# Autocorrelation by spectra: weights at plain delays, outputs as even and odd parts, and a new order of ScalarE's and TensorE's calls

## The chip, the cores and the metric

The kernel runs on one core of a Trainium2 chip. The metric is device microseconds of one execution, the median over several. TensorE does the matrix products and writes to PSUM; VectorE and ScalarE read PSUM and SBUF; GpSimd (POOL) works on SBUF only; SyncE (SP) issues the transfers. Each engine runs its own queue of instructions in order, and waits on semaphores where the program says so.

## The reference, cut to what matters

Two blocks in a row, each an attention-like step and a feed-forward step with a gate, over x of shape (8, 256, 1024). The change touches the second attention step only, an autocorrelation over time, on the normed x as query and on the context as key and value:

```python
corr = ifft(fft(q, axis=time) * conj(fft(k, axis=time))).real
topk = int(2 * np.log(L))                    # L = 256, topk = 11
w, idx = jax.lax.top_k(corr.transpose(0, 1, 3, 2), topk)
w = softmax(w)
for i in range(topk):
    g = jnp.minimum(idx[:, :, None, :, i] + pos, L - 1)
    out = out + w[:, :, None, :, i] * take_along_axis(v, g, axis=2)
x = x + tanh(g_xattn[1]) * out
x = x + tanh(g_ffn[1]) * ffn(layernorm(x))    # a 1024x1024 linear with a gain
```

For each channel the 11 largest correlations over the 256 delays become softmax weights, and the output is the value series, weighted at those delays. The shift is not circular: past the end the last value stands.

## The kernel before, in words

X (the running x) lies in SBUF in 16 tiles of 128 time rows by 1024 channels; a batch is two tiles, and the rows of its second tile are stored in reverse. With that, cosine and sine transforms over 256 time points split into a sum part and a difference part of 128 rows each.

The last phase, `phase_tail`, holds the second attention step and the last linear layer. It cuts the attention into N = 16 units (8 batches, two halves of 512 channels). Its main loop runs n from 0 to N + LAG - 1 = 18. In step n, unit n is at its output, unit n+1 at its correlation and selection, unit n+2 at its query and key spectra, and unit n+3 at its key's fold; beside these, tile `nxt` = n-2 of X is normed and turned and tile `now` = n-3 goes through the linear layer. Each engine has its own list of calls for a step; these lists are the order, written out by hand.

The calls that matter, by engine:

- TensorE (list at L1438 to L1466): `weight_turn(n)` transposes the softmax weights into psC (L1379); `linear(now, 0)` is 24 f16 matmuls of 512 columns (L1427); `weight_even(n)` takes the even spectrum of the weights, six f16 matmuls (high and low parts, L1338); `corr(n+1)`, 16 f32 matmuls of 256 columns (L1372); `weight_odd(n)`; `linear(now, 1)`; `turn(nxt, 0)`, four transposes into the first bank of psL (L1413); `k_odd(n+1)`, two f32 matmuls of 512 columns (L1334); `output(n)`, eight f32 matmuls of 512 columns from four sources into the two banks of psQ (L1401); `k_even(n+2)`; `turn(nxt, 1)` into the same bank of psL as the first turn; `q_spectrum(n+2)` into psQ (L1338). A f32 matmul shows as two records.
- VectorE (L1594 to L1628): `products(n+1)`, `weights_low(n)`, statistics, `weight_products(n, 0)` (e_d, e_x), `gain_of(now, 0)`, `weight_products(n, 1)` (n_d, n_x, L1572 and L1573), `select(n+1)` (the 11 largest by `max` and `match_replace`, L1537 to L1556; the instruction nmax at L1545; four masked products that sum the exponentials, L1560; the reciprocal, L1565), `gain_of(now, 1)`, `low(nxt, 0)` (L1503, reads the bank that the turn wrote), `add(n)` (X plus output times gate, L1579), `low(nxt, 1)`, `k_fix(n+3)` (L1515, L1517).
- ScalarE (L1306 to L1329): `weights_T`, `q_norm`, `corr_row`, `q_high`, `out_row`, `normed(nxt)`, `high(nxt, 0)` (L1294), `exps(n+1)`, `odd_out(n+1)`, `weights(n+1)` (four scalings by the reciprocal, L1269), `even_out(n+2)`, `high(nxt, 1)`.
- GpSimd (L1209 to L1232): `corr_comb`, `q_fold`, `out_comb(n, 0)`, `q_low`, `out_comb(n, 1)` (L1181, L1183), `add(now, 0)` (L1196), `k_fold(n+3)` (L1158, L1160), `w_fold(n+1)` (four sums and differences of weights, L1191), `add(now, 1)`.

Four waits tie them. `turn(d, half)` waits until the low copy of the previous half is made (L1406: `l_lo` of 2d + half), because both halves use one bank. `low` waits for `high` of the same half. `q_spectrum(n+2)` waits for `x_done`, the add of unit n, since both use psQ (L1358). `weights(n+1)` waits for the reciprocal and for w_fold (L1266, L1268).

The weights are folded before they are turned: weight at delay p plus or minus weight at delay 255 - p, so that the transform of 256 delays needs one product of 128 rows per spectrum part. The output is made by eight products, four spectrum parts for each of the two tiles.

Of the kernel before, what the change touches and what calls it, by code (L numbers as in the profile page):

```python
# [19 lines left out]
F32 = mybir.dt.float32  # L20
# [490 lines left out]
def phase_nf4_ffn(nc, io, res):  # L511
# [13 lines left out]
    with ExitStack() as ctx:  # L525
# [88 lines left out]
        with nc.Block() as block:  # L614
            @block.sync
            def _(sp):
# [43 lines left out]
                for name in ("fwd", "fwd_hi", "fwd_lo", "inv"):  # L660
                    sp.dma_start(res[name], io[name]).then_inc(res["const_in"], 16)
# [345 lines left out]
def spectra():  # L1007

    t, f = np.arange(P)[:, None] + 0.5, np.arange(P)[None, :]
# [4 lines left out]
    scaled = fwd * DFT_SCALE  # L1016
    high = scaled.astype(np.float16)
# [3 lines left out]
    weight = np.where(f == 0, 1.0, 2.0) / L  # L1021
    im_inv = -np.sin(even) * weight
    im_inv[:, :1] = (nyquist - 1.0) / L
    inv = np.stack([np.cos(even) * weight, im_inv, np.cos(odd) * 2 / L, -np.sin(odd) * 2 / L])
    return fwd.astype(np.float32), high, (scaled - high).astype(np.float16), inv.transpose(2, 0, 1).astype(np.float32)


def phase_tail(nc, io, res):
# [11 lines left out]
    with ExitStack() as ctx:  # L1040
# [6 lines left out]
        fwd, fwd_hi, fwd_lo, inv, const_in, ctx_in = (res[k] for k in ("fwd", "fwd_hi", "fwd_lo", "inv", "const_in", "ctx_in"))  # L1047
# [12 lines left out]
        wf = sb("wf", [P, 2, CH, P])  # L1060
        wT_hi, wT_lo = res["wT_hi"], res["wT_lo"]
# [22 lines left out]
        ex_done, w_done, rws_done, wf_done, wn_done = (sem(n) for n in ("ex_done", "w_done", "rws_done", "wf_done", "wn_done"))  # L1084
        wT_mm, wT_done, ws_mm, wprod_done, wprod_comb, out_mm, x_done = (sem(n) for n in ("wT_mm", "wT_done", "ws_mm", "wprod_done", "wprod_comb", "out_mm", "x_done"))
        wprod_row = sem("wprod_row")
# [20 lines left out]
        with nc.Block() as block:  # L1107
# [28 lines left out]
            def _(pool):  # L1136
# [71 lines left out]
                w_fold(0)  # L1208
# [26 lines left out]
            def _(act):  # L1235
# [70 lines left out]
                for n in range(N + LAG):  # L1306
# [25 lines left out]
            def _(pe):  # L1332
# [42 lines left out]
                def weight_turn(n):  # L1375
                    for c in range(CH):
                        pe.wait_ge(wn_done, CH * n + c + 1)
                        for h in range(2):
                            mm = pe.transpose(psC[:, h, c * P:(c + 1) * P], wf[:, h, c, :], ident[:])  # L1379
                    mm.then_inc(wT_mm, 1)  # L1380

                def weight_even(n):
                    pe.wait_ge(wTlo_done, n + 1)
                    pe.wait_ge(k_done, min(n + 2, N))
                    for half in range(2):
                        mm = dft_parts(psE, half, half, wT_hi[:, half, :], wT_lo[:, half, :])
                    mm.then_inc(ws_mm, 1)

                def weight_odd(n):
                    pe.wait_ge(wprod_done, 4 * n + 2)  # L1390
                    for half in range(2):
                        mm = dft_parts(psE, half, 2 + half, wT_hi[:, 1 - half, :], wT_lo[:, 1 - half, :])
                    mm.then_inc(ws_mm, 1)
# [364 lines left out]
```

## Time and profile before

| what | value |
|---|---|
| median of 3 runs | 2140.28 us (2139.77 to 2141.79) |
| the profiled execution | 2142.46 us |
| its span in the trace | 2140.7 us |
| TensorE clock, mean share of full over the span | 0.981 |
| TensorE busy | 2043.1 us, 95% |
| VectorE busy | 1100.8 us, 51% |
| ScalarE busy | 1175.7 us, 55% |
| GpSimd busy | 665.7 us, 31% |
| the last phase begins at about | 1594 us |
| SP issues the first context and the four constants at | 1558.5 to 1561.1 us, 0.4 to 0.6 us each |
| a context load of 1 MB, from issue to landing, median | 7.0 us |

Times in rows are microseconds from the start of the span unless marked ns. PE is TensorE's matmul, PEld its weight load, DVE VectorE, ACT ScalarE, POOL GpSimd, SP SyncE. A matmul's own duration runs past the start of the next one; the distance of starts is what a call costs. Where rows name xT_hi or xT_lo as operands, these are places in that large buffer, which in the last phase hold the constants, the context, the turned weights and the linear layer's weights.

### The profile page before, as it was taken

To read this page: it belongs to the slowest core of one execution; us is meant where nothing else is said; L and a number is where in the kernel's file an instruction comes from. 1 tells how busy PE (TensorE), PEld (TensorE's weight loads), DVE (VectorE), ACT (ScalarE), POOL (GpSimd) and SP (SyncE) were. 2 spreads that over 40 slices of the span, in tenths; PEclk is the share of its full clock that TensorE was granted. 3 is DMA by queue.
4 is the path that set the end of the run, shared out by engine and by line. 5 is a ranking of instruction groups with operands and counts; after the bars stand their busy time and mean duration, and the time that the engine had idled before them with its cause. 6 is when DMAs were issued, how large, how long until landed. Compare 5 with 4: busy or idle time off the path is not lost. (4 is left out here: it accounts for less than half of the span.)

```text
span 2140.7 us, 25963 instructions
## 1 busy us (share of the span) xinstructions
PE 2043.1 (95%) x9634; PEld 1022.6 (48%) x9634; DVE 1100.8 (51%) x1951; ACT 1175.7 (55%) x1851; POOL 665.7 (31%) x640
## 2 busy tenths in 40 slices
PE   7985999999999999999999999999986799999998
PEld 5773444444444444444444444444433455555544
DVE  5775252442624326243352523426257888888872
ACT  6994756656566565655656656565613344434431
POOL 3432211112121121211212111121226666776742
PEclk9997999999999999999999999999997899999999
DMA  6641211112122121121211111111040011101001
GB/s 218 201 137 63 77 50 60 46 49 75 50 75 70 55 69 55 60 69 56 69 55 60 50 55 50 50 55 50 30 148 10 30 40 50 49 36 50 26 20 40
DMA packets 65070, 136.77 MB, mean 64 GB/s; under 512 B 9008, under 2 KB 13744, under 8 KB 64944
## 3 DMA queue, kind: packets, MB, share of 16 engines
q1 hardware_dynamic: 64944, 135.11, 19.5%
q8 instruction: 77, 1.26, 0.2%
q14 instruction: 49, 0.40, 0.1%
HBM read 122.49 MB, written 12.58 MB: 63 GB/s over the span
## 5 line engine op out<-in xcount | busy, mean ns | idle before, releaser
L682 ACT ACTIVATE first<-first 128x512 f32<-128x512 int32 x1008 | 632.7, 628 | 28.0
L920 PE MATMUL ps_ring<-xT_hi,gu_hi 128*128 128x512 f16 x1376 | 522.4, 380 | 1.7 <-POOL gu_lo L758 1.7
L920 PE MATMUL ps_ring<-xT_lo,gu_hi 128*128 128x512 f16 x1376 | 522.2, 379 | 0.0
L920 PE MATMUL ps_ring<-xT_hi,gu_lo 128*128 128x512 f16 x1376 | 522.1, 379 | 0.0
L812 DVE SCALAR_TENSOR_TENSOR wt<-first,w_scale,absm 128x512 f32<-128x512 f32 x132 | 98.8, 749 | 478.4 <-ACT first L682 477.4
L758 POOL TENSOR_TENSOR gu_lo<-wt,gu_hi 128x512 f16<-128x512 f32 x88 | 102.6, 1166 | 763.8 <-ACT gu_hi L688 763.8
L831 DVE SCALAR_TENSOR_TENSOR X<-ps_ring,ffn_gain,X 128x512 f32<-128x512 f32 x352 | 259.8, 749 | 135.3 <-PE ps_ring L943 135.3
L943 PE MATMUL ps_ring<-dn_hi,hid_hi 128*128 128x512 f16 x704 | 266.9, 379 | 0.0
L943 PE MATMUL ps_ring<-dn_hi,hid_lo 128*128 128x512 f16 x704 | 266.8, 379 | 0.0
L943 PE MATMUL ps_ring<-dn_lo,hid_hi 128*128 128x512 f16 x672 | 254.6, 379 | 0.0
L920 PEld LDWEIGHTS ps_ring<-xT_hi,gu_hi 128*128 128x128 f16 x1376 | 134.7, 98 | 170.7 <-issue 12.7
L920 PEld LDWEIGHTS ps_ring<-xT_hi,gu_lo 128*128 128x128 f16 x1376 | 134.6, 98 | 163.0 <-issue 0.8
L697 ACT ACTIVATE rel<-ps_ring 128x512 f32<-128x512 f32 x84 | 50.1, 596 | 295.0 <-PE ps_ring L920 295.0
L920 PEld LDWEIGHTS ps_ring<-xT_lo,gu_hi 128*128 128x128 f16 x1376 | 134.7, 98 | 156.9 <-issue 0.8
L1427 PE MATMUL a_psL<-xT_lo,l_x 128*128 128x512 f16 x768 | 170.8, 380 | 2.5 <-DVE l_x L1503 2.5
L825 DVE SCALAR_TENSOR_TENSOR rel<-ps_ring,hid_gain,rel 128x512 f32<-128x512 f32 x84 | 63.1, 751 | 201.1 <-ACT rel L697 201.1
L688 ACT ACTIVATE gu_hi<-wt 128x512 f16<-128x512 f32 x88 | 55.1, 626 | 192.9 <-DVE wt L815 192.9
L758 POOL TENSOR_TENSOR dn_lo<-wt,dn_hi 128x512 f16<-128x512 f32 x42 | 48.5, 1156 | 349.3 <-ACT dn_hi L688 349.3
L1427 PEld LDWEIGHTS a_psL<-xT_lo,l_x 128*128 128x128 f16 x768 | 75.1, 98 | 90.5 <-DVE l_x L1503 2.9
L943 PEld LDWEIGHTS ps_ring<-dn_hi,hid_lo 128*128 128x128 f16 x704 | 68.8, 98 | 83.2
L815 DVE SCALAR_TENSOR_TENSOR wt<-ps_wide,lora_gain,wt 128x512 f32<-128x512 f32 x132 | 99.1, 751 | 14.8 <-PE ps_wide L902 10.2
L943 PEld LDWEIGHTS ps_ring<-dn_hi,hid_hi 128*128 128x128 f16 x704 | 68.8, 98 | 78.4
(207 smaller groups left out, 2686.4 us busy)
## 6 DMA issues: line engine op xcount, KB each, us to landing
first<-in_codes SPq DMA_DIRECT2D x132, 256.0 KB, 2.8
absm<-in_absmax SPq DMA_DIRECT2D x264, 128.0 KB, 3.0
X<-in_x SPq DMA_DIRECT2D x16, 512.0 KB, 4.7
c_in<-in_ctx SPq DMA_DIRECT2D x16, 512.0 KB, 5.6
cT<-in_ctxT SPq DMA_DIRECT2D x16, 512.0 KB, 3.6
xT_hi<-in_ctx SPq DMA_DIRECT2D x8, 1024.0 KB, 7.0
out<-X SPq DMA_DIRECT2D x15, 512.0 KB, 2.6
wide<-in_w SPq DMA_DIRECT2D x8, 512.0 KB, 4.7
```

The costliest lines, as they stand in the source:

```text
L682: act.activation(level[u % 2][:], codes[u % RING] if k == 0 else level[u % 2][:], ACT.Prelu, bias=bias, scale=scale, alpha=alpha).then_inc ...
L688: act.activation(dest(u, 0), wt[u % 2][:], ACT.Copy).then_inc(whi_done, 1)
L697: act.activation(rel[t % 2][:], ps_ring[2 + 2 * (t % 2)][:], ACT.Relu).then_inc(rel_done, 1)
L758: pool.tensor_tensor(dest(u, 1), wt[u % 2][:], dest(u, 0), ALU.subtract).then_inc(wlo_done, 1)
L812: dve.scalar_tensor_tensor(wt[u % 2][:], source[:], w_scale[:, m:m + 1], absm[u % RING][:], ALU.mult, ALU.mult).then_inc(scaled, 1)
L815: dve.scalar_tensor_tensor(wt[u % 2][:], ps_lora[u % 2][:], lora_gain[:, m:m + 1], wt[u % 2][:], ALU.mult, ALU.add).then_inc(wt_done, 1)
L825: dve.scalar_tensor_tensor(rel[t % 2][:], ps_ring[3 + 2 * (t % 2)][:], hid_gain[:], rel[t % 2][:], ALU.mult, ALU.mult).then_inc(mul_done, 1)
L831: dve.scalar_tensor_tensor(dst, ps_ring[n % 6][:], ffn_gain[:], dst, ALU.mult, ALU.add).then_inc(acc_done, 1)
L920: mm = pe.matmul(o[:], w[c][:, m, k, :], xx[:, k, ts], start=(q == 0), stop=(q == 3 * KD - 1))
L943: mm = pe.matmul(ps_ring[n % 6][:], hh[c][:, i * P:(i + 1) * P], w[c][:, hf * BANK:(hf + 1) * BANK], start=(q == 0), stop=(q == len(split) ...
L1427: mm = pe.matmul(out, a[:, ks], w[:, half * CH:(half + 1) * CH, k, :], start=(q == 0), stop=(q == 3 * KD - 1))
```

## The change

- The weights are no longer folded: `w_fold` is gone, `weights` scales `cut` (256 delays) in place, and `weight_turn` transposes its two halves. Each spectrum part now sums two products of 128 delays, so `weight_even` and `weight_odd` are twelve f16 matmuls each, with new constants `delay_hi` and `delay_lo`.
- `output` makes an even part and an odd part in place of the two tiles: four f32 matmuls with the constant `back`. VectorE adds the even part to both tiles. ScalarE copies the odd part out of PSUM, scaled by the gate (`anti_out`), and GpSimd adds it to one tile and subtracts it from the other (`anti_add`). GpSimd corrects one row of e_d first (`dc_fix`).
- Order: on ScalarE `anti_out(n)` and `weights(n+1)` stand ahead of `high(nxt, 0)`; on TensorE `k_odd(n+1)` and `output(n)` stand ahead of `turn(nxt, 0)`; on VectorE `add(n)` stands ahead of `low(nxt, 0)`. On GpSimd `anti_add(n-1)` opens step n.
- Three more constants are loaded, two get smaller; `wT_lo` moves to a buffer of its own.

```diff
@@ SP, before the phase
-                for name in ("fwd", "fwd_hi", "fwd_lo", "inv"):
+                for name in ("fwd", "fwd_hi", "fwd_lo", "inv", "back", "delay_hi", "delay_lo"):
                     sp.dma_start(res[name], io[name]).then_inc(res["const_in"], 16)
@@ GpSimd
-                def w_fold(n):
-                    if n:
-                        pool.wait_ge(wT_mm, n)
-                    for c in (0, 2):
-                        pool.wait_ge(w_done, CH * n + c + 2)
-                        for k, op in enumerate((ALU.add, ALU.subtract)):
-                            pool.tensor_tensor(wf[:, k, c:c + 2, :], cut[:, c:c + 2, 0:P], cut[:, c:c + 2, P:L][:, :, ::-1], op).then_inc(wf_done, 1)
+                def dc_fix(n):
+
+                    pool.wait_ge(wprod_comb, 4 * n + 1)
+                    pool.tensor_tensor(e_d[0:1, 0, :], e_d[0:1, 0, :], e_d[0:1, 1, :], ALU.subtract).then_inc(dc_done, 1)
+
+                def anti_add(n):
+                    pool.wait_ge(anti_done, n + 1)
+                    for t, op in enumerate((ALU.add, ALU.subtract)):
+                        pool.wait_ge(sym_done, 2 * n + t + 1)
+                        dst = X[:, 2 * (n // 2) + t, cols(n)]
+                        pool.tensor_tensor(dst, dst, anti[:], op).then_inc(x_done, 1)
...
                 for n in range(N + LAG):
                     now = tile(n - LAG)
+                    if 0 < n <= N:
+                        anti_add(n - 1)
...
                     if n < N:
                         out_comb(n, 1)
+                        dc_fix(n)
...
-                    if n + 1 < N:
-                        w_fold(n + 1)
@@ ScalarE
                     for c in range(CH):
-                        act.wait_ge(wf_done, 4 * n + 2 * (c // 2) + 2)
-                        act.activation(wf[:, :, c, :], wf[:, :, c, :], ACT.Copy, scale=rws[:, c:c + 1]).then_inc(wn_done, 1)
+                        act.activation(cut[:, c, :], cut[:, c, :], ACT.Copy, scale=rws[:, c:c + 1]).then_inc(wn_done, 1)
+
+                def anti_out(n):
+                    act.wait_ge(anti_mm, n + 1)
+                    if n:
+                        act.wait_ge(x_done, 2 * n)
+                    act.activation(anti[:], psQ[:, 1, :], ACT.Copy, scale=half_gate[:]).then_inc(anti_done, 1)
...
                     if nxt is not None:
                         normed(nxt)
-                    if nxt is not None:
-                        high(nxt, 0)
                     if n + 1 < N:
                         exps(n + 1)
                         odd_out(n + 1)
+                    if n < N:
+                        anti_out(n)
+                    if n + 1 < N:
                         weights(n + 1)
+                    if nxt is not None:
+                        high(nxt, 0)
@@ TensorE
                 def q_spectrum(n):
                     pe.wait_ge(qlo_done, n + 1)
                     if n >= 2:
-                        pe.wait_ge(x_done, 2 * n - 2)
+                        pe.wait_ge(sym_done, 2 * n - 2)
+                        pe.wait_ge(anti_done, n - 1)
...
+                def weight_spectrum(k):
+                    for half in range(2):
+                        for q, (w, src) in enumerate(((delay_hi, wT_hi), (delay_hi, wT_lo), (delay_lo, wT_hi))):
+                            for h in range(2):
+                                mm = pe.matmul(psE[:, half, :], w[:, 2 * k + half, h, :], src[:, h, :], start=(q + h == 0), stop=(q + h == 3))
+                    mm.then_inc(ws_mm, 1)
...
-                    for half in range(2):
-                        mm = dft_parts(psE, half, half, wT_hi[:, half, :], wT_lo[:, half, :])
-                    mm.then_inc(ws_mm, 1)
+                    weight_spectrum(0)
...
                 def output(n):
                     pe.wait_ge(prod_done, min(2 * n + 4, 2 * N))
                     pe.wait_ge(wprod_row, n + 1)
-                    for k, src in enumerate((e_d, e_x, n_d, n_x)):
-                        pe.wait_ge(wprod_comb, 4 * n + k + 1)
-                        for t in range(2):
-                            mm = pe.matmul(psQ[:, t, :], inv[:, k, t * P:(t + 1) * P], src[:, 0, :], start=(k == 0), stop=(k == 3))
-                    mm.then_inc(out_mm, 1)
+                    pe.wait_ge(wprod_comb, 4 * n + 2)
+                    pe.matmul(psQ[:, 1, :], back[:, 1, :], e_x[:, 0, :], start=True, stop=False)
+                    pe.wait_ge(wprod_comb, 4 * n + 3)
+                    pe.matmul(psQ[:, 1, :], back[:, 2, :], n_d[:, 0, :], start=False, stop=True).then_inc(anti_mm, 1)
+                    pe.wait_ge(wprod_comb, 4 * n + 4)
+                    pe.matmul(psQ[:, 0, :], back[:, 3, :], n_x[:, 0, :], start=True, stop=False)
+                    pe.wait_ge(dc_done, n + 1)
+                    pe.matmul(psQ[:, 0, :], back[:, 0, :], e_d[:, 0, :], start=False, stop=True).then_inc(out_mm, 1)
...
                     if now is not None:
                         linear(now, 1)
-                    if nxt is not None and n < N:
-                        turn(nxt, 0)
                     if n + 1 < N:
                         k_odd(n + 1)
                     if n < N:
                         output(n)
+                    if nxt is not None and n < N:
+                        turn(nxt, 0)
@@ VectorE
                     for t in range(2):
                         dst = X[:, 2 * (n // 2) + t, cols(n)]
-                        dve.scalar_tensor_tensor(dst, psQ[:, t, :], half_gate[:], dst, ALU.mult, ALU.add).then_inc(x_done, 1)
+                        dve.scalar_tensor_tensor(dst, psQ[:, 0, :], half_gate[:], dst, ALU.mult, ALU.add).then_inc(sym_done, 1)
...
                         gain_of(now, 1)
+                    if n < N:
+                        add(n)
                     if nxt is not None and n < N:
                         low(nxt, 0)
-                    if n < N:
-                        add(n)
```

## Rows read from the trace of the kernel before

**Rows 1.** Busy time by stretch: us, PE, PEld, DVE, ACT, POOL busy (x), PEclk, DMA share, GB/s

```profile
1839.00:1869.00 30.00, 30.00 (x127) 15.93 (x125) 25.98 (x58) 12.28 (x19) 21.64 (x21) 1.00 0.20 63
1637.00:1665.00 28.00, 22.69 (x66) 11.62 (x66) 20.73 (x50) 10.35 (x17) 16.98 (x15) 0.86 0.06 14
```

**Rows 2.** Line L1545, all steps, then 1720 to 2060: ns min/median/max, first and last start

```profile
L1545 DVE TENSOR_SCALAR nmax<-top x16: 169/1084/1110, 1625.1 to 2065.7; 128x4 f32<-128x4 f32 x16
...
L1545 DVE TENSOR_SCALAR nmax<-top x11: 811/1094/1110, 1737.4 to 2036.0; 128x4 f32<-128x4 f32 x11
```

**Rows 3.** Timeline of TensorE around step 7: start, us, instructions, idle before and releaser

```profile
1844.79 1.46 PE L1338 MATMUL a_psE<-xT_hi 128*128 128x512 f16 x6
1846.08 0.59 PE L1372 MATMUL a_psC<-xT_hi,t_d 128*128 128x256 f32 x2
...
1849.59 1.47 PE L1338 MATMUL a_psE<-xT_hi 128*128 128x512 f16 x6
1850.90 5.34 PE L1427 MATMUL a_psL<-xT_lo,l_x 128*128 128x512 f16 x24
...
1858.23 1.88 PE L1401 MATMUL a_psQ<-e_d,xT_hi 128*128 128x512 f32 x4
...
1865.10 1.02 PE L1334 MATMUL a_psE<-xT_hi 128*128 128x512 f32 x2
...
1866.82 0.60 PE L1413 MATMUL a_psL<-ident,l_xn 128*128 128x128 f32 x4
1867.25 0.38 PE L1338 MATMUL a_psQ<-q_hi,xT_hi 128*128 128x512 f16 x1
...
1868.55 1.04 PE L1379 MATMUL a_psC<-ident,wf 128*128 128x128 f32 x8
1869.42 5.34 PE L1427 MATMUL a_psL<-xT_lo,l_x 128*128 128x512 f16 x24
1874.60 1.46 PE L1338 MATMUL a_psE<-xT_hi 128*128 128x512 f16 x6
```

**Rows 4.** Timeline of VectorE in step 7

```profile
1851.17 1.23 DVE L1572 TENSOR_TENSOR n_d<-a_psE,o_sp 128x1024 f32<-128x1024 f32 x1 [0.96 <-PE a_psE L1338]
...
1861.04 0.87 DVE L1560 SCALAR_TENSOR_TENSOR cut<-cut,ex 128x256 f32<-128x256 f32 x1
...
1862.19 0.41 DVE L1560 SCALAR_TENSOR_TENSOR cut<-cut,ex 128x256 f32<-128x256 f32 x1
...
1862.53 0.94 DVE L1560 SCALAR_TENSOR_TENSOR cut<-cut,ex 128x256 f32<-128x256 f32 x1
...
1863.51 0.18 DVE L1565 RECIPROCAL rws<-wsum 128x4 f32<-128x4 f32 x1
...
1865.30 1.41 DVE L1579 SCALAR_TENSOR_TENSOR X<-a_psQ,half_gate,X 128x512 f32<-128x512 f32 x2 [0.42 <-PE a_psQ L1401]
```

**Rows 5.** GpSimd in step 7, and line L1517 of VectorE over all steps

```profile
1856.56 1.26 POOL L1183 TENSOR_TENSOR n_x<-n_x 128x512 f32<-128x512 f32 x1
...
1862.41 3.01 POOL L1191 TENSOR_TENSOR wf<-cut 128x256 f32<-128x256 f32 x4 [0.78 <-DVE cut L1560]
...
L1517 DVE SCALAR_TENSOR_TENSOR xT_hi<-xT_hi x16: 691/692/1633, 1598.1 to 2019.4; 128x512 f32<-128x512 f32 x16
```

**Rows 6.** Timeline of ScalarE in step 7

```profile
1864.14 0.91 ACT L1269 ACTIVATE wf<-wf,rws 128x256 f32<-128x256 f32 x2 [3.78 <-POOL wf L1191]
...
1867.93 0.59 ACT L1294 ACTIVATE l_x<-a_psL 128x512 f16<-128x512 f32 x1
```

**Rows 7.** TensorE after two pauses, and the stretch behind the first (columns as in rows 1)

```profile
2085.53 2.74 PE L1338 MATMUL a_psE<-xT_hi 128*128 128x512 f16 x6 [2.53 <-DVE e_x L1573]
2088.07 5.67 PE L1427 MATMUL a_psL<-xT_lo,l_x 128*128 128x512 f16 x24
...
2103.15 5.36 PE L1427 MATMUL a_psL<-xT_lo,l_x 128*128 128x512 f16 x24 [1.67 <-DVE l_x L1503]
...
2085.00:2087.00 2.00, 1.47 (x4) 0.59 (x5) 1.31 (x3) 0.05 (x1) 1.92 (x2) 0.58 0.00 0
```

More of the change, by code:

```diff
@@ L1015, in spectra @@
     fwd = np.stack([np.cos(even), even_im, np.cos(odd), -np.sin(odd)]).transpose(1, 0, 2)
-    scaled = fwd * DFT_SCALE
-    high = scaled.astype(np.float16)
+    weight = np.where(f == 0, 1.0, 2.0) / L
+    back_im = even_im * weight
+    back_im[:, :1] = np.sin(np.pi * t) / L
+    back = np.stack([np.cos(even) * weight, back_im, np.cos(odd) * 2 / L, -np.sin(odd) * 2 / L]).transpose(2, 0, 1)
     t = np.arange(L)[:, None]
@@ L1020, in spectra @@
     nyquist = np.where(t % 2 == 0, 1.0, -1.0)
-    weight = np.where(f == 0, 1.0, 2.0) / L
     im_inv = -np.sin(even) * weight
     im_inv[:, :1] = (nyquist - 1.0) / L
-    inv = np.stack([np.cos(even) * weight, im_inv, np.cos(odd) * 2 / L, -np.sin(odd) * 2 / L])
-    return fwd.astype(np.float32), high, (scaled - high).astype(np.float16), inv.transpose(2, 0, 1).astype(np.float32)
+    inv = np.stack([np.cos(even) * weight, im_inv]).transpose(2, 0, 1)
+    delay_im = -np.sin(even)
+    delay_im[:, :1] = -nyquist
+    delay = np.stack([np.cos(even), delay_im, np.cos(odd), -np.sin(odd)]).reshape(4, 2, P, P).transpose(2, 0, 1, 3)
+    scaled = [fwd[:, :2] * DFT_SCALE, delay * DFT_SCALE]
+    high = [m.astype(np.float16) for m in scaled]
+    low = [(m - h).astype(np.float16) for m, h in zip(scaled, high)]
+    return {"fwd": fwd.astype(np.float32), "inv": inv.astype(np.float32), "back": back.astype(np.float32),
+            "fwd_hi": high[0], "fwd_lo": low[0], "delay_hi": high[1], "delay_lo": low[1]}
 def phase_tail(nc, io, res):
@@ L1045, in sem @@
             return ctx.enter_context(nc.semaphore("a_" + name))
-        fwd, fwd_hi, fwd_lo, inv, const_in, ctx_in = (res[k] for k in ("fwd", "fwd_hi", "fwd_lo", "inv", "const_in", "ctx_in"))
+        fwd, fwd_hi, fwd_lo, inv, back, delay_hi, delay_lo = (res[k] for k in ("fwd", "fwd_hi", "fwd_lo", "inv", "back", "delay_hi", "delay_lo"))
+        const_in, ctx_in = res["const_in"], res["ctx_in"]
         c_in = [res[f"ctx_in{s}"] for s in range(2)]
@@ L1384, in weight_even @@
                     pe.wait_ge(k_done, min(n + 2, N))
-                    for half in range(2):
-                        mm = dft_parts(psE, half, half, wT_hi[:, half, :], wT_lo[:, half, :])
-                    mm.then_inc(ws_mm, 1)
+                    weight_spectrum(0)
                 def weight_odd(n):
                     pe.wait_ge(wprod_done, 4 * n + 2)
-                    for half in range(2):
-                        mm = dft_parts(psE, half, 2 + half, wT_hi[:, 1 - half, :], wT_lo[:, 1 - half, :])
-                    mm.then_inc(ws_mm, 1)
+                    weight_spectrum(1)
                 def output(n):
@@ L1429, in linear @@
                     mm.then_inc(lin_mm, 1)
-                pe.wait_ge(const_in, 64)
+                pe.wait_ge(const_in, 112)
                 k_even(0)
@@ L1539, in select @@
                     if n:
-                        dve.wait_ge(wf_done, 4 * n)
+                        dve.wait_ge(wT_mm, n)
                     settle(dve)
@@ L1643, in build @@
         place, start = res["xT_hi"][:].rearrange("p k t -> p (k t)"), 0
-        for name, shape, dt in (("ctx_in0", [2, D], F32), ("ctx_in1", [2, D], F32), ("fwd", [4, P], F32), ("inv", [4, L], F32), ("last", [BANK], F32),
-                                ("fwd_hi", [4, P], HALF), ("fwd_lo", [4, P], HALF), ("wT_hi", [2, BANK], HALF), ("wT_lo", [2, BANK], HALF)):
+        for name, shape, dt in (("ctx_in0", [2, D], F32), ("ctx_in1", [2, D], F32), ("fwd", [4, P], F32), ("inv", [2, L], F32), ("back", [4, P], F32), ("last", [BANK], F32),
+                                ("fwd_hi", [2, P], HALF), ("fwd_lo", [2, P], HALF), ("delay_hi", [4, 2, P], HALF), ("delay_lo", [4, 2, P], HALF), ("wT_hi", [2, BANK], HALF)):
             size = int(np.prod(shape)) * (2 if dt is F32 else 1)
@@ L1729, in layouts @@
     bound_q = np.stack([s.reshape(P, -1) for s in (*absmax_of, np.pad(a["L0_ffn_d_absmax"], ((0, 0), (0, padf // QBLK))))], 1)
-    fwd, fwd_hi, fwd_lo, inv = spectra()
     arrays = {
@@ L1734, in layouts @@
         "w1": a["L1_ffn_W"].reshape(KD, P, D).transpose(1, 0, 2),
-        "fwd": fwd, "fwd_hi": fwd_hi, "fwd_lo": fwd_lo, "inv": inv,
+        **spectra(),
         "x": a["x"], "ctx": a["ctx_4096"],
```

11 lines of the change are left out of this document (5 added, 6 removed).

## The prediction, made before the changed kernel ran

> **What bounds the kernel now.** I read the stretches first, because the change lies in the last phase only. In its steady part TensorE is busy 30.00 of 30 us at full clock, while in the first steps it is busy 22.69 of 28 us and its clock averages 0.86 [rows 1]. So three quarters of the phase's steps are bound by TensorE's own work, and the rest by waits. One row gives the period: the nmax instruction of VectorE stands 11 times between 1737.4 and 2036.0, ten periods of 29.86 us [rows 2].
>
> Then I read TensorE's queue over one step (n = 7) [rows 3]. Row starts give each call's price: linear(., 1) 5.18 us, turn 0.43, k_odd and k_even 1.72 each, output 6.87 (1858.23 to 1865.10), q_spectrum 1.30, weight_turn 0.87, weight_even 1.29, corr 3.45 (1846.08 to 1849.59 less a wake of 0.06), weight_odd 1.31. With the second linear and turn they sum to 29.8: no wait is left.
>
> VectorE, though, is close behind [rows 4]. From n_d at 1851.17 (0.27 us after linear(., 1) starts on TensorE at 1850.90) it runs without a gap to the reciprocal, done at 1863.69, 12.52 us later, then gain, low, and at 1865.30 the add, done at 1866.71. TensorE needs that add only at 1867.25 [rows 3]: the slack is half a microsecond. The question is what becomes of it.
>
> **The change, part by part.** Times t below count from the start of linear(., 1).
>
> 1. Output: four f32 matmuls of 512 columns in place of eight. 6.87 us become 3.44. Off TensorE's path: 3.43.
> 2. Weight spectra: twelve f16 matmuls instead of six, twice a step. Six take 1.29, so 2.58 are added. The net on TensorE is -0.85 a step, 28.95 in place of 29.8.
> 3. w_fold goes from GpSimd (3.01 us for four, beginning 0.1 us before VectorE's last masked product) [rows 5]. ScalarE's scaling no longer waits for it, but in the steady part TensorE did not wait for the scaling, so this alone gives nothing there.
> 4. GpSimd gets two X adds and dc_fix. Each costs about what the row of n_x costs, 1.26 for 512 elements [rows 5]. dc_fix has 512 elements in one partition only; no row tells whether that is cheaper, so I take 1.26 and bound it by 0.2. GpSimd has 3.0 us less and 3.8 more of 30, busy 21.6 now [rows 1]. dc_fix comes behind n_x and before output needs it (n_x done near t = 4, output's last product at t = 9.5), so it costs nothing. Were GpSimd 4 us later, TensorE would wait.
> 5. ScalarE gets anti_out, 0.6 us like a high copy [rows 6], for which output's first half is early enough (t = 8.6); it hides in the wait for the reciprocal.
> 6. VectorE's two adds keep number and shape; that both read one bank costs nothing (bound 0 to 0.1).
> 7. **The moved copies.** high(nxt, 0) now stands behind weights(n+1) on ScalarE. Behind high stands low(nxt, 0) on VectorE, behind that turn(nxt, 1) on TensorE (it overwrites the bank that low reads), and behind that, in TensorE's queue, q_spectrum and the whole next step. Before, this copy ran early, since turn(nxt, 0) did.
> 8. SP issues three constants more, about 0.5 us each, for 0.4 MB net; its constants go out more than 30 us before the phase begins, and 1 MB of context beside them lands in 7 us (table ahead). The cost is nothing, since the rest of the layer before covers it; uncovered it would be 2 us.
>
> **The sum for one step.** TensorE is ready for turn(nxt, 1) at t = 15.92 before (1850.90 to 1866.82) and at 15.92 - 3.43 = 12.49 after. VectorE's chain is not shortened by that. The reciprocal ends at 0.27 + 12.52 = 12.79 less what select gains. What it gains: nmax takes 1.09 in the median of the steady part and 0.17 at the least anywhere [rows 2]; the first and last masked product take 0.87 and 0.94 against 0.41 for a middle one [rows 4]. The long ones overlap GpSimd instructions: nmax lies beside n_x's at 1856.56, the last product beside w_fold [rows 5]. With w_fold gone the last one gives back 0.52 surely. nmax and the first depend on where GpSimd's adds fall: 0 to 1.4. I take 1.2 in all, bounds 0.5 and 1.9. Then ScalarE: a wake of 0.1, four scalings at 0.43 apart (1.75), high 0.59 [rows 6]; VectorE: low 0.68, two wakes of 0.05. 12.79 - 1.2 + 2.44 + 0.78 = 14.8. TensorE starts turn(nxt, 1) at 14.8 and not at 12.5: it stands still 2.3 us. (The add's route is shorter: 12.7 - 1.2 + 0.6 + 1.41 + 0.1 = 13.6.)
>
> From turn(nxt, 1) to the next linear(., 1) TensorE needs 0.43 + 1.30 + 0.87 + 5.18 + 1.29 + 3.45 + 1.31 = 13.83 now and 16.41 after, with the spectra doubled. weight_odd's wait for e_x is covered by corr (2.5 under 3.45), weights_low by linear(., 0). Period 14.8 + 16.4 = 31.2 against 29.86: +1.35 a step, over the 11 steady steps +15 us; with the bounds +7 and +23.
>
> Here a rule of the skill is to be weighed. The rows show that a VectorE instruction with operands in SBUF grows when GpSimd runs beside it: L1517 takes 0.69, at most 1.63 [rows 5]. The Trainium skill, SBUF — State Buffer, section "SBUF: two separate sides", says of the shared port pair that whoever starts first keeps it for the whole instruction and the other is blocked, if VectorE has two SBUF inputs and GpSimd reads SBUF. By that rule the trace agrees (the long ones above), and it speaks against this change too: the new adds of X fall upon k_fix. From rows: up to 0.9 us for each of two, against a slack of about 1.1: TensorE is free for weight_even at t = 14.8 + 0.43 + 1.30 + 0.87 + 5.18 = 22.6, and VectorE has by then the second low (16.7, behind turn and its high), two k_fix (18.1), two products and weights_low, each as long as n_d (21.5). I take it as covered; if both collide in every step it is +0.7 a step, 8 us, inside the upper bound.
>
> **The clock.** Six pauses of TensorE of 2.5 to 3.1 us that began at clock 1.00 were each followed by a stretch at half rate (1.2 of 2.4 GHz), as at 2085.53 after 2.53 us: granted 0.58, six matmuls in 2.74 instead of 1.46, and the 24 behind them 5.67 instead of 5.34 [rows 3, 7]. That is 1.6 us lost. After the pause of 1.67 us before 2103.15 the same 24 took 5.36: no drop [rows 7]. The new pause of 2.3 lies between, nearer to those that drop. The loss falls on turn, q_spectrum, weight_turn and linear(., 0), all on the cycle. I take 8 of 12 steps: +13 us. Bounds 0 and 20.
>
> **The ends.** Steps 0 and 1 have no turns: TensorE is bound there by weight_odd, select, add, and the doubled spectra eat what output gives back, +0.3 each. Before step 0 nothing covers w_fold, and what of its 3.0 us [rows 5] the scalings do not overlap, with the port waits, comes off: -1.8. Step 2 is like a steady one but loses its wait for l_xn: +0.2. Step 14 has neither k_even nor q_spectrum to fill the pause: +3. In step 15 output is 3.44 shorter and no scaling precedes the copy: -1.9. Sum 0, bounds -4 and +4.
>
> Total 15 + 13 + 0 = +28 us. The profiled execution (2142.46; span 2140.7 and 1.8 around it) would go to 2170; it lies 2.2 above the median of 2140.28, so the forecast is **2168 us**.
>
> **The rivals.**
> - The pause comes, but the clock holds 1.00: 2140.3 + 15 = 2155 (2148 to 2163). For it: the pause is shorter than any that dropped. Against: only 0.2 us shorter than the shortest of them. Chance 0.22.
> - **The other side, faster:** TensorE stays the bound, and 0.85 a step is gained: 11 x 0.85 = 9.4, with the start's 1.8 and step 15's 1.9, 2127 us. Its place is low(nxt, 0), which would have to be done by t = 12.5; the price of the chain would have to fall by 2.3 beside the 1.2 that I granted. All three port waits together give 1.9. It decides only if the chain from n_d to the reciprocal were under 9 us. Chance 0.06.
> - The change does next to nothing: all 1.9 us of port waits go, the clock holds, and the ends come out at their lower bound: 11 x 0.65 - 4 = +3, 2143 us. Chance 0.06.
> - The pause exceeds 3 us or two half-rate stretches follow (k_fix blocked, select not shorter): 23 + 20 + 8, 2190 us or more. Chance 0.08.
>
> **How the numbers follow.** The forecast's own case, steps of which most drop, has 0.58 and spans 2156 to 2187. With the first rival that is 0.80, so the range is 2147 to 2187. A measurement of this kernel can tell about 0.2% (4.3 us) from no change. Faster than 2136: 0.06. Within: 0.06. Slower: 0.88, from the forecast, the first and the last rival.
>
> **What would show it.** In the profile after: TensorE's row of turn with about 2.3 us idle before it in every step, released by VectorE's low; four scalings right behind the reciprocal and high right behind them; nmax about 31 to 33 us apart; clock under 1.00 after many pauses; the last masked product at 0.41; output's four rows in 3.44. Wrong, if TensorE's rows are back to back at 28.95 a step, if low(nxt, 0) starts before the reciprocal is done, or if the clock stays 1.00.

## The result, and the profile after

The kernel after the change takes **2168.08 us** (median of 4 runs, 2166.59 to 2171.91) against 2140.95 us before (4 runs): a ratio of 1.0124, 95% interval 1.0112 to 1.0136. It is 1.2% slower, and the forecast was 2168. The profiled execution took 2171.91 us with a span of 2170.1, so it lies 3.8 above the median; its span is 29.4 longer than the one of before.

Busy time by stretch, first a steady stretch and the first steps, as [rows 1], then two short pieces around one pause (columns as there):

```profile
1872.00:1902.00 30.00, 28.16 (x124) 14.98 (x122) 25.13 (x59) 12.38 (x20) 20.82 (x20) 1.00 0.07 27
1637.00:1665.00 28.00, 22.34 (x70) 10.99 (x70) 19.88 (x48) 9.89 (x18) 17.96 (x14) 0.82 0.01 4
1787.00:1789.00 2.00, 0.10 (x1) 0.00 (x0) 1.65 (x3) 2.00 (x5) 2.00 (x2) 1.00 0.07 27
1789.00:1793.00 4.00, 3.81 (x17) 2.72 (x18) 2.53 (x5) 0.83 (x2) 1.50 (x2) 0.66 0.29 120
```

TensorE was busy 30.00 of 30 us; now 28.16. It has become an engine that waits, once a step. The last two lines show what one such wait may bring: a gap at clock 1.00, then 4 us at a mean of 0.66, that is, mostly at 1.2 in place of 2.4 GHz. Such a stretch is called half rate below.

TensorE's queue over the same step as in [rows 3]:

```profile
1869.47 5.34 PE L1456 MATMUL a_psL<-xT_lo,l_x 128*128 128x512 f16 x24
...
1876.37 1.02 PE L1425 MATMUL a_psQ<-e_x,xT_hi 128*128 128x512 f32 x2
...
1879.80 0.60 PE L1442 MATMUL a_psL<-ident,l_xn 128*128 128x128 f32 x4
...
1881.10 1.02 PE L1356 MATMUL a_psE<-diff,xT_hi 128*128 128x512 f32 x2
1883.96 0.63 PE L1442 MATMUL a_psL<-ident,l_xn 128*128 128x128 f32 x4 [1.84 <-DVE l_x L1532]
...
1886.59 5.34 PE L1456 MATMUL a_psL<-xT_lo,l_x 128*128 128x512 f16 x24
...
1900.40 0.81 PE L1456 MATMUL a_psL<-xT_lo,l_x 128*128 128x512 f16 x3
```

Output takes 3.43 us (1876.37 to 1879.80) in place of 6.87. TensorE could start its next call at 1881.96, 12.49 us after the start of linear(., 1), and starts it at 1883.96. (Pauses are given below as the rows have them, 1.84 here; that is counted from the end of the last matmul and so a little shorter than the distance of starts.) From that turn to the next linear(., 1) it needs 16.44.

What it waited for, on VectorE, as [rows 4]; then ScalarE, as [rows 6]; then GpSimd, as [rows 5]:

```profile
1869.74 1.22 DVE L1601 TENSOR_TENSOR n_d<-a_psE,o_sp 128x1024 f32<-128x1024 f32 x1 [2.74 <-PE a_psE L1409]
...
1875.32 0.68 DVE L1574 TENSOR_SCALAR nmax<-top 128x4 f32<-128x4 f32 x1
...
1880.23 0.42 DVE L1589 SCALAR_TENSOR_TENSOR cut<-cut,ex 128x256 f32<-128x256 f32 x1
...
1880.69 0.18 DVE L1594 RECIPROCAL rws<-wsum 128x4 f32<-128x4 f32 x1
...
1881.38 1.40 DVE L1608 SCALAR_TENSOR_TENSOR X<-a_psQ,half_gate,X 128x512 f32<-128x512 f32 x2
1883.12 0.69 DVE L1532 SCALAR_TENSOR_TENSOR l_x<-a_psL,l_x 128x512 f16<-128x512 f32 x1 [0.35 <-ACT l_x L1313]
```

```profile
1880.90 1.71 ACT L1282 ACTIVATE cut<-cut,rws 128x256 f32<-128x256 f32 x4 [1.80 <-DVE rws L1594]
1882.51 0.57 ACT L1313 ACTIVATE l_x<-a_psL 128x512 f16<-128x512 f32 x1
```

```profile
1873.49 1.26 POOL L1198 TENSOR_TENSOR e_d<-e_d 1x512 f32<-1x512 f32 x1
1874.72 1.26 POOL L1210 TENSOR_TENSOR X<-X,l_prod 128x512 f32<-128x512 f32 x1
...
1883.85 2.50 POOL L1205 TENSOR_TENSOR X<-X,anti 128x512 f32<-128x512 f32 x2
```

Read upward from the turn at 1883.96: low ends at 1883.81, high at 1883.08, the scalings at 1882.61, the reciprocal at 1880.87, which is 11.13 us after n_d began (12.52 before). All masked products of this step take 0.41 or 0.42 now, since no w_fold lies beside the last one. One dc_fix, for one partition, takes 1.26, as long as 128 partitions.

nmax stands 11 times between 1749.4 and 2063.2, so the mean period is 31.38, against 29.86 in [rows 2]. The waits from 1735 to 2095 (total us, times, longest) show two links of the cycle. Below them stands the chain of the whole span by engine, which had 22% TensorE and 2% VectorE before:

```profile
L1574 DVE TENSOR_SCALAR nmax<-top x11: 170/690/973, 1749.4 to 2063.2; 128x4 f32<-128x4 f32 x11
```

```profile
PE a_psL L1442 <- DVE l_x L1532: 21.4, 11, 2.1
...
ACT cut L1282 <- DVE rws L1594: 20.1, 11, 2.2
```

```profile
PE 14%; DVE 8%; issue 3%; ACT 1%; POOL 0%; DVEq 0%; POOLq 0%; ACTq 0%
```

**Where the 29.4 us are.** From the starts of the 16 n_d in both traces (a step's interval is the distance to the next):

| part | before | after | difference |
|---|---|---|---|
| up to the phase's first instruction (a_st) | 1594.23 | 1598.50 | +4.3 |
| from there to n_d of step 0 | 51.49 | 51.35 | -0.1 |
| steps 0 and 1 | 27.67, 27.48 | 30.52, 30.81 | +6.2 |
| step 2 | 30.90 | 32.60 | +1.7 |
| steps 3 to 13 | 328.39 | 344.76 | +16.4 |
| step 14 | 28.22 | 29.61 | +1.4 |
| from n_d of step 15 to the end | 52.32 | 51.95 | -0.4 |

The first line is not the change: SP issues the first context at 1562.75 in place of 1558.49, so that execution was late before anything of the change ran. In the nine profiles below that also load the three new constants, n_d of step 0 starts at 1644.1 to 1647.5, against 1649.85 here and 1645.72 before.

The second line hides two changes. From the phase's first instruction to weight_even of step 0 it takes 40.10 us in place of 43.20, since nothing waits for w_fold. From there to n_d it takes 11.25 in place of 8.29, since the doubled spectra stand there, the first at half rate.

In steps 3 to 13 the usual interval is 30.95 (+1.09 on 29.86). Two steps of 32.87 and 32.89 are 1.93 us longer: 0.25 from a longer pause, which two more steps have (31.2), and 1.67 from a half-rate stretch. Up to step 10 the turn's pauses alternate between about 1.85 and 2.1 us, in most steps because nmax alternates between 0.69 and 0.97. Of the four pauses of 2.09 to 2.12, two were followed by half rate; of those of 1.84 and 1.85, none. The turn of step 2 comes after 3.33 us and runs at half rate. The turn of step 14 comes after a pause as long, and there the clock held:

```profile
2102.77 0.63 PE L1442 MATMUL a_psL<-ident,l_xn 128*128 128x128 f32 x4 [3.57 <-DVE l_x L1532]
```

The same pause in e3, e4 and e6 (3.56 to 3.57) was followed by half rate, and step 14 took 31.9 and 32.3 in e4 and e6. So the 29.61 of the table owe some 2.5 us to the clock of this one execution.

Steps 0 and 1 were forecast at +0.3 each. VectorE, GpSimd and TensorE there:

```profile
1662.24 1.39 DVE L1544 SCALAR_TENSOR_TENSOR xT_hi<-xT_hi 128x512 f32<-128x512 f32 x1
1663.67 1.65 DVE L1546 SCALAR_TENSOR_TENSOR xT_hi<-xT_hi 128x512 f32<-128x512 f32 x1
1665.24 1.21 DVE L1558 TENSOR_TENSOR t_d<-a_psQ,k_sp 128x1024 f32<-128x1024 f32 x1
```

```profile
1661.81 2.95 POOL L1205 TENSOR_TENSOR X<-X,anti 128x512 f32<-128x512 f32 x2 [4.31 <-DVE X L1608]
```

```profile
1668.77 1.03 PE L1409 MATMUL a_psE<-xT_hi 128*128 128x512 f16 x2 [4.01 <-DVE wT_lo L1550]
```

The two k_fix take 1.39 and 1.65, against 0.69 alone, under anti_add. weight_even then comes after a pause of 4.01 us (2.71 before) and runs at half rate, two matmuls in 0.82 (to the next at 1669.59) where they need 0.43.

### The profile page after: what moved, and what is told of

It is laid out like the page before. It is cut to its first block and busy times, and to the rows that moved or that the text cites. A ratio compares the mean times of both kernels' runs of the same rounds, so it can differ in the third digit from the quotient of the medians.

```text
span 2170.1 us, 26094 instructions
## 1 busy us (share of the span) xinstructions
PE 2038.5 (94%) x9698; PEld 1018.5 (47%) x9698; DVE 1095.0 (50%) x1951; ACT 1182.0 (54%) x1867; POOL 677.9 (31%) x624
## 3 DMA queue, kind: packets, MB, share of 16 engines
q8 instruction: 77, 1.26, 0.2%
```

## The experiments

All expectations below were on record before the run. Ratios are to the kernel before on the same chip; its medians there were 2141.64 us (e1 to e4), 2142.0 (e5 to e8) and 2141.22 (e9 to e11). The theory: the new order closes a cycle (reciprocal, scalings, high, low, turn, next step) that sets the period. The rivals: the doubled spectra alone, or the clock, or the port of SBUF. "Interval" is the distance of two n_d.

### The order alone (e1, e2)

e1 is the kernel after with the three orders of before; e2 is the kernel before with the three orders of the change, nothing else. The edit of e1 (e2 is its mirror):

```diff
@@ ScalarE
+                    if nxt is not None:
+                        high(nxt, 0)
                     if n + 1 < N:
                         exps(n + 1)
...
                         weights(n + 1)
-                    if nxt is not None:
-                        high(nxt, 0)
@@ TensorE
                         linear(now, 1)
+                    if nxt is not None and n < N:
+                        turn(nxt, 0)
...
                         output(n)
-                    if nxt is not None and n < N:
-                        turn(nxt, 0)
@@ VectorE
-                    if n < N:
-                        add(n)
                     if nxt is not None and n < N:
                         low(nxt, 0)
+                    if n < N:
+                        add(n)
```

> The changed kernel with the three orders of before: turn(nxt, 0) ahead of k_odd and output, high(nxt, 0) ahead of exps, low(nxt, 0) ahead of add. Theory (the steady cycle runs n_d, select, reciprocal, scalings, high, low, turn(nxt, 1), q_spectrum): low is early again, and q_spectrum waits for the add alone, which ends 13.6 us after n_d, so q_spectrum starts at 13.7 in place of 14.7. Period 29.95 us in place of 30.95, pauses near 1 us, clock 1.00; 11 steps and the two ends: about 2153 us. Rival (the moved copies cost nothing, the selection or TensorE's work alone sets the period): period 30.95, 2168 us.

Measured: 2151.41 us, 1.0044 [1.0029, 1.0059]. Step 2 takes 29.36 in place of 32.60, a steady step 30.44, the stretch behind n_d of step 15 49.26 in place of 51.95, and no steady step drops the clock. Steps 0 and 1, in which no tile is turned, are as long as after the change (30.57, 30.85). The pause before the turn is short:

```profile
1811.76 0.63 PE L1442 MATMUL a_psL<-ident,l_xn 128*128 128x128 f32 x4 [0.50 <-DVE l_x L1532]
```

> The kernel before with the three order changes alone; folded weights and eight output products stay. Theory: the scalings end 15.2 us after n_d (they still wait for w_fold), then high 0.6 and low 0.7, so turn(nxt, 1) starts 16.5 after n_d and not 15.65: a pause of 0.9 us a step, period 30.75 in place of 29.86, about 2152 us, clock 1.00. Rival (the order is harmless or helps): 2141 us or less.

Measured: 2148.03 us, 1.0029 [1.0019, 1.0039], a steady interval of about 30.3 (+0.45; +0.9 was expected). The reciprocal came 12.1 us after n_d in most steps, and not 12.5, since nmax fell to 0.69 or 0.76. The turn, which waits for nothing in the kernel before, now waits once a step:

```profile
1838.26 0.63 PE L1413 MATMUL a_psL<-ident,l_xn 128*128 128x128 f32 x4 [0.41 <-DVE l_x L1503]
```

So the order costs 16.7 us in the kernel after (2168.1 less 2151.4) and 6.4 in the kernel before. The parts do not add: 6.4 and e1's 9.8 make 16, and both together cost 27. In e1's interval of 30.44 the turn is no longer the link. q_spectrum waits there for the two adds, which come behind a reciprocal of 11.54 us after n_d (first masked product 0.66, nmax 0.78 in the median). I had put that at 11.13, hence 29.95; 0.5 too low.

### The doubled spectra and the shorter output (e3, e4)

e3 leaves out the second 128 delays of the weights in the spectra, six matmuls in place of twelve. e4 keeps the kernel after and runs k_even's two matmuls twice, 1.72 us more of TensorE, placed before the pause.

```diff
@@ e3
-                            for h in range(2):
-                                mm = pe.matmul(psE[:, half, :], w[:, 2 * k + half, h, :], src[:, h, :], start=(q + h == 0), stop=(q + h == 3))
+                            mm = pe.matmul(psE[:, half, :], w[:, 2 * k + half, 0, :], src[:, 0, :], start=(q == 0), stop=(q == 2))
@@ e4
+                    if n >= 4:
+                        dft(0, 0, raw(n)[:, 1, cols(n)])
+                        dft(1, 1, diff[n % 2][:])
                     dft(0, 0, raw(n)[:, 1, cols(n)])
```

> The changed kernel with the six f16 matmuls of before in each weight spectrum: the second 128 delays are left out of the weights' transform. Theory: both spectra lie on the cycle between turn(nxt, 1) and n_d, so the period falls by their whole 2.58 us, to 28.4, and the first steps by 2.6 or more each: about 2127 us, though TensorE still pauses 2 us a step. Rival (TensorE pauses anyway, so its work is hidden): the pause grows to 4.6 us, period 30.95, 2168 us or more.

Measured: 2142.88 us, 1.0003 [0.9991, 1.0014]: 16 above what was expected, though undisturbed intervals are 28.37, 28.32 and 28.34, 2.6 under 30.95, with pauses of 1.8 to 1.9 us as after the change. But four of the eleven steady steps take 32.8 to 33.1. TensorE's pause there is 3.63 to 3.66 us, since nmax (1.10) and two masked products (0.74 and 1.47) grow beside GpSimd, and half rate follows. The turn, and the 4 us around it (columns as in [rows 1]):

```profile
1774.39 1.09 PE L1441 MATMUL a_psL<-ident,l_xn 128*128 128x128 f32 x4 [3.63 <-DVE l_x L1531]
```

```profile
1774.00:1778.00 4.00, 3.61 (x11) 2.01 (x12) 2.07 (x4) 1.02 (x2) 1.69 (x2) 0.50 0.34 135
```

So the added matmuls are wholly on the path, 2.58 a step, and at the full price only because they lie behind the pause: what output saves lies ahead of it. In total e3 is 25 us below the kernel after and e1 17, of 27 in all. The two causes overlap: either of them taken away gives back more than half of the loss.

> The changed kernel with the two matmuls of k_even run twice from step 2 on (same operands, same result): 1.72 us of work more for TensorE, just ahead of the pause before turn(nxt, 1). Theory: the pause of 2.0 us takes it up whole, period stays 30.95, and the clock has no pause left that drops it (two of the eleven steady steps of the profile took 1.9 us longer at half rate): 2164 us, between 2160 and 2169. Rival (TensorE's work sets the period): 12 x 1.72 = 21 us more, 2189 us.

Measured: 2166.05 us, 1.0114 [1.0099, 1.0129]. Four matmuls in place of two (to 1783.29), and the intervals are still 30.94 to 31.2:

```profile
1780.72 1.02 PE L1356 MATMUL a_psE<-diff,xT_hi 128*128 128x512 f32 x2
1781.58 1.02 PE L1356 MATMUL a_psE<-xT_hi 128*128 128x512 f32 x2
...
1783.86 0.63 PE L1445 MATMUL a_psL<-ident,l_xn 128*128 128x128 f32 x4 [0.40 <-DVE l_x L1535]
```

1.72 us of added work cost nothing; they took the pause's place, and no steady step is at 32.9. So at least that half of output's saved 3.43 us bought nothing: it had become the wait. It also answers the rival that the loss is the clock's: with no half rate in the steady steps the kernel is 2 us faster, not 27.

### The first steps and the port (e5, e6)

e5 leaves out dc_fix, so the correction of one row is missing. e6 puts anti_add behind corr_comb in steps 1 and 2, so that it does not fall upon k_fix.

```diff
@@ e5
                         out_comb(n, 1)
-                        dc_fix(n)
...
-                    pe.wait_ge(dc_done, n + 1)
@@ e6
-                    if 0 < n <= N:
+                    late = n < 3
+                    if 0 < n <= N and not late:
                         anti_add(n - 1)
...
                         corr_comb(n + 1)
+                    if 0 < n <= N and late:
+                        anti_add(n - 1)
```

> The changed kernel without dc_fix: the correction of one row of e_d is left out. Theory (dc_fix took 1.26 us on GpSimd and pushes the X add behind it under nmax, which then takes 0.68 us and not 0.17): the X add ends 1.26 earlier, nmax is free, 0.5 us a step less on the cycle, period 30.45, about 2162 us. Rival (as predicted, dc_fix is hidden and costs nothing): 2168 us.

Measured: 2165.29 us, 1.011 [1.0095, 1.0125]. nmax takes 0.17 in steady steps and yet the interval is 30.91: moving GpSimd's queue earlier freed nmax and put k_fold upon the next masked product (0.85 in place of 0.41). All pauses of the steady steps are now 1.4 to 1.8 us and none is followed by half rate, so steps 3 to 13 are 5.2 us shorter in this profile. Steps 0 and 1 take 28.7 and 29.43, that is 3.2 less, but step 14, at half rate, takes 31.82. The rows of VectorE, then GpSimd's k_fold:

```profile
1743.52 0.17 DVE L1572 TENSOR_SCALAR nmax<-top 128x4 f32<-128x4 f32 x1
...
1746.92 0.85 DVE L1587 SCALAR_TENSOR_TENSOR cut<-cut,ex 128x256 f32<-128x256 f32 x1
```

```profile
1746.22 1.27 POOL L1170 TENSOR_TENSOR xT_hi<-xT_hi 128x512 f32<-128x512 f32 x1
```

> The changed kernel with GpSimd's anti_add behind corr_comb in steps 1 and 2 only. Theory (in the first steps, where no linear layer covers VectorE, anti_add lies under the two k_fix, which take 3.0 us from start to products and not 1.4): the two first intervals between n_d shrink by 1.6 us each, from 30.5 and 30.8 to about 29, total 2165 us. Rival (the slow start is the doubled spectra at half clock alone): intervals unchanged, 2168 us.

Measured: 2164.69 us, 1.0105 [1.009, 1.012]. The intervals of steps 0 and 1 are 28.17 and 27.15 (before 27.67 and 27.48); step 2 gives 1.6 back (34.15). k_fix is short again:

```profile
1658.95 0.68 DVE L1547 SCALAR_TENSOR_TENSOR xT_hi<-xT_hi 128x512 f32<-128x512 f32 x1
1659.67 0.69 DVE L1549 SCALAR_TENSOR_TENSOR xT_hi<-xT_hi 128x512 f32<-128x512 f32 x1
```

The pauses before weight_even are 2.71 again, in place of 4.01 and 4.08; the first is followed by half rate, the second is not. So the 6.2 us of steps 0 and 1 come from anti_add on k_fix and the half rate behind the pause that it lengthens. What dc_fix has to do with them stays open: in e5 the reciprocal comes 0.43 and 0.47 us sooner there, but k_fix is as long as before (1.39 and 1.65) and the pauses stay at 4.01 and 4.08. The other 2.3 of e5's 3.2 us are a half rate that ended sooner behind the same pauses.

### Select ahead of the odd products (e7, e8, e9)

If the theory holds, the chain from n_d to the reciprocal can be shortened by running select's four `max` and first four `match_replace` before n_d and n_x, where VectorE waits anyway (2.74 us before n_d). e8 does the same to the kernel before. e9 is e7 with k_fold behind the linear layer's second add.

```diff
@@ e7, e8: VectorE
                     if n < N:
+                        if n + 1 < N:
+                            select_top(n + 1)
                         weight_products(n, 1)
                     if n + 1 < N:
-                        select(n + 1)
+                        select_rest(n + 1)
@@ e9: GpSimd
-                    if n + 3 < N:
-                        k_fold(n + 3)
                     if now is not None:
                         add(now, 1)
+                    if n + 3 < N:
+                        k_fold(n + 3)
```

> The changed kernel with the first part of select (four max, four match_replace, 3.3 us) ahead of weight_products(n, 1) on VectorE, where it idles 2.7 us for weight_odd. Theory: the reciprocal comes about 1.9 us earlier (2.7 less 0.6 by which n_d starts later and some port waits), the pause before turn(nxt, 1) all but closes, period 28.95 to 29.1, at TensorE's own work; the first steps gain 2 us each: about 2137 us. Rival (something else than the selection's place holds the chain): 2168 us.

Measured: 2154.45 us, 1.0063 [1.0046, 1.008]. The interval is about 30.45 in most steps, half a microsecond less and not 1.9. The freed time went into the port: three masked products under k_fold. VectorE, then GpSimd:

```profile
1770.91 0.75 DVE L1591 SCALAR_TENSOR_TENSOR cut<-cut,ex 128x256 f32<-128x256 f32 x1
...
1771.59 1.47 DVE L1591 SCALAR_TENSOR_TENSOR cut<-cut,ex 128x256 f32<-128x256 f32 x1
...
1773.00 1.48 DVE L1591 SCALAR_TENSOR_TENSOR cut<-cut,ex 128x256 f32<-128x256 f32 x1
```

```profile
1771.34 1.44 POOL L1168 TENSOR_TENSOR diff<-xT_hi 128x512 f32<-128x512 f32 x1
1772.86 1.33 POOL L1170 TENSOR_TENSOR xT_hi<-xT_hi 128x512 f32<-128x512 f32 x1
```

> The kernel before with the same split of select. Theory (before, TensorE's work sets the period of 29.86 us, so an earlier selection buys nothing in the steady part, and in the first steps the add waits for output's products anyway): 2140 us, 2137 to 2142. Rival (the split is worth its 2 us in any kernel): 11 x 1.9 less, 2120 us.

Measured: 2149.3 us, 1.0037 [1.0024, 1.005], a miss. The steady steps are unchanged (328.2), as expected of a stretch that TensorE bounds. Steps 0 to 2 take 30.36, 30.54 and 31.92, 6.8 us more (step 14 gives 2.0 back): nothing covers the wait there, n_x comes later, and k_odd and output stand behind it and run at half rate:

```profile
1650.22 2.05 PE L1334 MATMUL a_psE<-diff,xT_hi 128*128 128x512 f32 x2 [4.55 <-DVE n_x L1575]
```

> The kernel of the split select (on the changed kernel) with GpSimd's k_fold(n+3) behind add(now, 1). Theory (the split gave 0.5 us a step in place of 1.9 because k_fold then lay under the masked products, three of which took 0.75, 1.47 and 1.48 us in place of 0.41): with k_fold out of the way only the first is long, the reciprocal comes 2.1 us earlier, the pause of 1.5 us before turn(nxt, 1) closes, and the period is TensorE's own work, 28.95 to 29.1: 11 x 1.5 = 16 us less than the 2154.5 of the split, 2138 us. Rival (the scalings and the moved copies hold the chain, not the port): 2154 us.

Measured: 2143.33 us, 1.0011 [1.0002, 1.0021], 11 below e7 and 5 above what was expected. With k_fold off the masked products, the reciprocal comes 8.0 us after n_d (9.9 in e7), and the interval alternates between 29.3 and 30.2; in every second step TensorE now waits 0.6 to 1.0 us for weights_low.

### The edits together (e10, e11)

e10 is the kernel after with four edits shown above: the orders of before (e1), the split select from step 2 on (e7), k_fold late (e9), anti_add late in steps 1 and 2 (e6). e11 is e10 with the change's orders.

```diff
                     if n < N:
+                        if n + 1 < N and n >= 2:
+                            select_top(n + 1)
                         weight_products(n, 1)
+                        if n + 1 < N and n < 2:
+                            select_top(n + 1)
```

> The changed kernel with what the runs point to: the three orders of before, select split from step 2 on only, k_fold(n+3) behind add(now, 1), anti_add behind corr_comb in steps 1 and 2. Theory: the three intervals of n_d at the start 28.2, 27.2 and 29.4, then 11 steps of 29.0 (TensorE's work, clock 1.00), the end as with the old order: about 2130 us, 11 us faster than the kernel before. Rival (the chain over VectorE sets the period in any order, near 29.9 or more): 2141 us or more.

Measured: **2136.29 us** (11 runs), 0.9979 [0.997, 0.9988]: 0.2% faster than before and 1.5% than after. Not 2130: in every second step the two k_fix still fall under anti_add, and weight_even waits. The wait from 1735 to 2050, and one of it:

```profile
PE a_psE L1412 <- DVE wT_lo L1553: 6.6, 10, 1.2
```

```profile
1811.83 0.61 PE L1412 MATMUL a_psE<-xT_hi 128*128 128x512 f16 x2 [1.11 <-DVE wT_lo L1553]
```

```profile
1805.13 1.51 DVE L1547 SCALAR_TENSOR_TENSOR xT_hi<-xT_hi 128x512 f32<-128x512 f32 x1
1806.67 1.64 DVE L1549 SCALAR_TENSOR_TENSOR xT_hi<-xT_hi 128x512 f32<-128x512 f32 x1
```

```profile
1804.82 2.94 POOL L1205 TENSOR_TENSOR X<-X,anti 128x512 f32<-128x512 f32 x2
```

Against the profiled execution of before its span is 6.2 us shorter: 2.2 in steps 3 to 13, 1.2 in step 14, 3.1 behind the last n_d, 0.6 in steps 0 to 2, less 0.9 ahead of n_d of step 0.

> The same as e10_best but with the three orders of the change. Theory: in the steady part the reciprocal is early enough for both orders (turn(nxt, 1) is due 11.7 us after n_d, low ends near 11.5), so the period is 29.0 there too; step 2 keeps its pause at half clock, 32.6 against 29.4, and the two last steps 3 us: about 2136 us. Rival (the moved copies cost 0.5 us a step whatever the selection does): 2141 us.

Measured: 2142.28 us, 1.0007 [0.9998, 1.0015], 6 above e10 and above what was expected. The number is the rival's, the mechanism is not: steps 3 to 13 are equal (326.5 against 326.2). Once VectorE's chain is short, the order costs nothing in the steady part, only its ends: 0.7 in step 2 and 2.8 behind the last n_d. Another 1.3 lies in steps 0 and 1 (26.90 and 30.97 against 28.17 and 28.36), where nothing is turned and both kernels make the same calls, so it is not the order's; half rate falls differently in the two executions.

## Why the prediction was right, and where it was not

By its own steps, against the profiled execution of after:

| term of the sum (t from the start of linear(., 1)) | forecast | measured |
|---|---|---|
| TensorE ready for the second turn, t | 12.49 | 12.49 |
| what select gains | 1.2 | 1.39 |
| start of the second turn, t | 14.8 | 14.49 |
| from it to the next linear(., 1) | 16.41 | 16.44 |
| 11 steady steps, without clock | +15 | +12.0, and 1.0 for four longer pauses |
| clock | +13 (8 of 12 steps at 1.6) | +3.4 (2 of 11 at 1.67; step 2 in its own row) |
| steps 0 and 1 | +0.6 | +6.2 |
| step 2 / 14 | +0.2 / +3 | +1.7 / +1.4 |
| start / step 15 | -1.8 / -1.9 | -0.1 / -0.4 |

**Right: the mechanism.** The moved copy closes a cycle through the reciprocal; e1 takes it away and the long pauses go, e4 fills the pause and costs nothing, e3 gives back the 2.58 of its matmuls in an undisturbed step. The faster rival needed low(nxt, 0) at t = 12.5; it was done at 14.34.

**Mis-sized: the clock.** "The new pause of 2.3 lies between, nearer to those that drop" took all pauses as one length. They are 1.84 to 2.12, because select gained 1.39 and the scalings, high and low together took 0.1 less, and at this length half rate followed only at times. The price of one such stretch was right (1.6 against 1.67), the count was not. The first rival (2155, the clock holds) was nearer in this term.

**Wrong: steps 0 and 1.** "The doubled spectra eat what output gives back, +0.3 each" left out the port there; with anti_add off k_fix (e6) the two steps are +0.2 together. The rule that the prediction weighed (the Trainium skill, SBUF — State Buffer, section "SBUF: two separate sides") was taken as covered by a slack of 1.1 us that was worked out for a steady step; the first steps have none. With that rule this trace agrees: k_fix at 1.39 and 1.65 beside anti_add, 0.68 with anti_add elsewhere (e6). In the steady step its cover held: 1.04 and 0.69, and TensorE did not wait for weights_low.

**Wrong in part: dc_fix "costs nothing".** Its duration was right (1.26, against a lower bound of 0.2), and its removal gives 0.04 in the usual steady interval. But it pushes GpSimd's next add onto nmax: 0.4 to 0.5 us in each of the first two steps, and in the steady part the longer pauses that half rate may follow (e5).

**Start and step 15**, -1.8 and -1.9, gave next to nothing. At the start the gain came and was larger, 3.1 us up to weight_even of step 0. What the sum left out is that unit 0's doubled spectra stand ahead of n_d of step 0 and took 3.0 of it back; in e3, without them, the way from the phase's first instruction to n_d is 48.86 and not 51.35. **Step 2 and step 14**, +0.2 and +3, came out at +1.7 and +1.4. The first is the order's: with the old one step 2 takes 29.36 (e1), with the new one its turn waits 3.33 us and half rate follows. The second had the clock on its side (above). In step 15 the pauses of 1.75 and 1.42 before the turn and the linear layer were followed by 24 matmuls in 7.04 us in place of 5.35, in which output's gain is lost.

So the total of 28 is partly luck: 12 too much on clock and period stood against 6 too little on steps 0 and 1 and 3 of gain at the start and in step 15 that did not come, and in the profiled execution 4.3 us ahead of the phase made up the rest. The medians differ by 27.1; how much of that lies ahead of the phase on average stays open.

## What to carry to other kernels

Before moving a step behind another in one engine's queue, follow what its result releases on every other engine: work saved on TensorE ahead of its wait is worth nothing once a chain through VectorE and ScalarE sets the period, and work added behind the wait counts in full. Cost the first and last steps of a software pipeline from their own rows, since a cover that holds in the steady part is not there. Where VectorE and GpSimd both work in SBUF, an instruction made earlier on either may fall beside another partner; list the overlaps again after each edit.

## What the runs showed of the hardware that was not expected

- **Half rate behind shorter pauses, and not behind every long one.** In the last phase of the kernel before, all pauses of 2.5 us and more that began at clock 1.00 were followed by it, and the one of 1.67 was not. Here two of four pauses of 2.09 to 2.12 were (one of four in e6, 2.10 to 2.13), and none of 1.84 or 1.85; in e7 one of 1.94 was. In e3, every pause of 3.57 to 3.66 was, and the one of 2.38, but not the one of 2.33; here one of 3.57 (step 14) and three of 2.53 to 2.62 (steps 1, 2 and 14) were not. The length of the pause alone does not decide it in these traces.
- **A GpSimd add on one partition costs what 128 cost**: 1.26 us for 1x512 and for 128x512.
- **Port time saved tends to come back.** nmax fell from 0.69 to 0.17 in e5 and the step by 0.04; in e7 a chain that was to be 1.9 us shorter made the step 0.5 shorter, with masked products at 0.75, 1.47 and 1.48 in place of 0.41.
